# Bias, first weights and first gate sums between the token stage and the head stage of an audio tower kernel

## The reference

```python
x = layer_norm(x, g1, b1)                 # 1472 rows of 1024
h = layer_norm(x @ W + b, g2, b2)         # 1472 rows of 512, the residual
n = layernorm(h)
q, k, v = n @ Wq, n @ Wk, n @ Wv          # 8 heads, 2 queries for each key, width 128
log_g = log_sigmoid(6.9 + n @ Wg)         # a gate per token and head
logG = cumsum(log_g, over the tokens)
a = where(causal, (q.k * scale) ** 2 * exp(logG[t] - logG[s]), 0)
y = (a @ v) / (sum(a) + 1e-6)
h = h + y @ Wc + bc
```

## Time and profile before

| what | value |
|---|---|
| median of 3 runs | 1456.67 us (1453.85 to 1457.67) |
| profiled execution, its own time | 1465.22 us |
| its span in the profile | 1463.4 us |
| mean granted TensorE clock | 0.928 of full speed |
| VectorE, ScalarE, GpSimd busy | 63%, 44%, 16% |
| longest chain, by engine | TensorE 57%, VectorE 23%, issue 11% |

### The profile page before, as it was taken

The page is one execution under the profiler, slowest core; times in us unless marked ns, Lnnn a source line. Parts: engine busy times, 40 slices in busy tenths (PEclk is TensorE's granted clock), DMA queues, the critical chain, the costliest instruction groups (busy, mean ns, idle before and its releaser), DMA issues.

```text
span 1463.4 us, 28621 instructions
## 1 busy us (share of the span) xinstructions
PE 1293.8 (88%) x9676; PEld 796.9 (54%) x9690; DVE 916.6 (63%) x1920; ACT 638.8 (44%) x1086; POOL 230.1 (16%) x280
## 2 busy tenths in 40 slices
PE   5999899999999999986759999999986798759997
PEld 2447667677676766765324444444533566424443
DVE  5983565666555566659744555544347666678886
ACT  3444444544444454444215444444523432236663
POOL 2220000000000000000013333333257610010000
PEclk9997999999999999996769999999997877889999
DMA  5212352433535244322215866876346510000000
GB/s 187 72 65 86 119 205 105 179 146 127 215 135 195 99 173 163 130 111 90 86 73 196 293 225 249 297 249 202 102 140 117 89 26 3 1 0 16 22 22 26
DMA packets 42700, 184.21 MB, mean 126 GB/s; under 512 B 8689, under 2 KB 9201, under 8 KB 34833
## 3 DMA queue, kind: packets, MB, share of 16 engines
q0 software_dynamic: 19744, 95.41, 19.6%
q1 hardware_dynamic: 19440, 75.41, 14.5%
q10 hardware_dynamic: 3456, 12.58, 2.5%
HBM read 135.65 MB, written 47.73 MB: 125 GB/s over the span
## 4 chain that ended last, share of the span: by engine, by line
PE 57%; DVE 23%; issue 11%; ACT 3%; DMA 2%; DVEq 2%; POOL 1%; another core or an unknown queue 1%; ACTq 0%; SPq 0%; POOLq 0%
PE ps L911 14%; PE ps L913 14%; PE ps L912 14%; PE ps L1017 3%; PE ps L996 3%; DVE ff L2017 2%; DVE amf L2024 1%; PE ps L1033 1%; DVE wa_lo L1381 1%; PE ps L1101 1%; PE ps L1352 1%; DVE bst L1454 1%; PE ps L1334 1%; DVE nrm L1746 1%; PE ps L1002 1%
## 5 line engine op out<-in xcount | busy, mean ns | idle before, releaser
L911 PE MATMUL ps<-nT_hi,wa_hi 128*128 128x368 f16 x576 | 189.2, 328 | 11.1 <-DVE wa_lo L1381 8.1
L912 PE MATMUL ps<-nT_lo,wa_hi 128*128 128x368 f16 x576 | 188.9, 328 | 0.0
L913 PE MATMUL ps<-nT_hi,wa_lo 128*128 128x368 f16 x576 | 188.3, 327 | 0.0
L657 ACT ACTIVATE qk<-ps 128x368 f32<-128x368 f32 x128 | 60.4, 478 | 128.8 <-PE ps L913 128.6
L1746 DVE SCALAR_TENSOR_TENSOR nrm<-ps,xg,nrm 128x256 f32<-128x256 f32 x61 | 29.5, 484 | 133.1 <-ACT nrm L725 112.1
L911 PE MATMUL ps<-wide,xT 128*128 x244 | 93.4, 383 | 12.7 <-issue 7.5
L500 POOL DMA_INDIRECT xg<-xrow,idx x61 | 61.3, 1004 | 276.0 <-PE ps L1101 106.6
L1574 DVE TENSOR_TENSOR a<-sq,E 92x368 f32<-92x368 f32 x64 | 32.6, 537 | 107.2 <-ACT sq L673 107.2
L1548 DVE SCALAR_TENSOR_TENSOR wide<-ps,wide 128x368 f32<-128x368 f32 x128 | 69.4, 542 | 48.5 <-PE ps L913 48.5
L912 PE MATMUL ps<-wide,xT 128*128 x244 | 93.1, 382 | 0.0
L913 PE MATMUL ps<-wide,xT 128*128 x244 | 93.0, 381 | 0.0
(11 more groups left out here) (312 smaller groups left out, 3097.5 us busy)
## 6 DMA issues: line engine op xcount, KB each, us to landing
we_st<-in_we POOLq DMA_DIRECT2D x16, 1536.0 KB, 6.7
wsp<-we_sp POOLq DMA_DIRECT2D x16, 1536.0 KB, 5.3
wide<-wsp SPq DMA_DIRECT2D x16, 1536.0 KB
yslot<-yt POOLq DMA_DIRECT2D x61, 256.0 KB
wq_st<-in_ffq SPq DMA_DIRECT2D x24, 512.0 KB, 4.5
wq_st<-in_ffq ACTq DMA_DIRECT2D x24, 512.0 KB
wide<-in_wa SPq DMA_DIRECT2D x10, 1024.0 KB, 6.3
xt<-in_x SPq DMA_DIRECT2D x12, 512.0 KB, 3.2
```

Source lines behind the costliest of these rows:

```text
L657: nc.scalar.activation(B["qk"][:, j, :], ps[:, j % 2, 0:CW], ACT.Copy, scale=(AS if j == 3 else 1.0) / WS).then_inc(b_ev, 1)
L911: nc.tensor.matmul(dst, lhs[0], rhs[0], start=start, stop=False)
L912: nc.tensor.matmul(dst, lhs[0], rhs[1], start=False, stop=False)
L913: return nc.tensor.matmul(dst, lhs[1], rhs[0], start=False, stop=stop)
```

## The change

SyncE gets one more wait: it goes into the loop of loads only when the first gr has landed. ScalarE's four bias activations go behind turns 12 and 13 of the token pipeline, two in each, and each now counts up acc_set, so that VectorE waits for 4 (KD) in place of 1; the first weights' high half goes behind turn 14. VectorE's low half of these weights goes behind its turn 14 also, that is ahead of turn 15 with the last block's `ln_low`. TensorE forms the running sums of the gates after one projection of the first head in place of two.

```diff
--- before.py
+++ after.py
@@ -404,6 +404,7 @@
             sp.dma_start(lgd.rearrange("h (a p) -> (h a) p", p=AT), B["lgt"][:, :]).then_inc(init_out, 16)
             sp.wait_ge(init_out, 32)
             sp.dma_start(B["gr"][0:AT], lgd[0:1, :].broadcast_to([AT, T])).then_inc(gr_in, 16)
+            sp.wait_ge(gr_in, 16)
             with sp.Fori(0, HEADS - 1) as i:
                 sp.wait_ge(q_abs, 3 * i + 1)
                 for m in range(3):
@@ -637,14 +638,14 @@
                                      bias=A["nb"][:, 4 + p:5 + p], scale=rt_out[:, 4 + p:5 + p]).then_inc(ln_nr, 1)
 
 
+            def biased(b0, b1):
+                act.wait_ge(ones_set, 3)
+                for blk in range(b0, b1):
+                    nc.scalar.activation(big[:, blk, :], big[:, blk, :], ACT.Identity,
+                                         bias=bcol[:, blk:blk + 1]).then_inc(acc_set, 1)
+
             pipeline(act, NT, [(1, tok_high), (4, lambda k, p, half: ln_high(k, k, 4 + p)), (0, x_norm), (3, h_norm)],
-                     after={0: tok_weights})
-
-            unit_a_hi(0)
-            act.wait_ge(ones_set, 3)
-            for blk in range(KD):
-                ins = nc.scalar.activation(big[:, blk, :], big[:, blk, :], ACT.Identity, bias=bcol[:, blk:blk + 1])
-            ins.then_inc(acc_set, 1)
+                     after={0: tok_weights, NT: lambda: biased(0, 2), NT + 1: lambda: biased(2, KD), NT + 2: lambda: unit_a_hi(0)})
             act.wait_ge(g_mm, 2)
             nc.scalar.activation(B["lt"][0:AT, 1, :], B["lt"][0:AT, 1, :], ACT.Exp, scale=-1.0).then_inc(g_ln, 1)
             act.wait_ge(g_ln, 1)
@@ -1038,13 +1039,13 @@
                 out_proj(g, c)
 
             pe.wait_ge(wa_lo, 1)
-            for j in range(2):
-                head_project(0, 0, j)
+            head_project(0, 0, 0)
             pe.wait_ge(g_lg, 1)
             nc.tensor.matmul(ps[0:AT, 7, 0:16 * HEADS], tri[0:AT, :], B["lg"][0:AT].rearrange("p a b -> p (a b)"),
                              start=True, stop=True)
             nc.tensor.matmul(ps[:, 6, 0:AT], B["lg"][0:AT].rearrange("p a b -> p (a b)"), tri[0:AT, :],
                              start=True, stop=True).then_inc(g_cum, 1)
+            head_project(0, 0, 1)
             with pe.Fori(0, HEADS - 1) as i:
                 head(i, False)
             head(HEADS - 1, True)
@@ -1517,9 +1518,8 @@
             pipeline(dve, NT, [(3, z_stats), (0, x_stats(0)), (3, z_moments), (0, x_stats(1)), (0, x_moments), (3, z_scaled),
                                (0, shift(0, rx_done, a_sx)), (3, h_row), (1, x_low(0)), (3, h_stats), (1, x_low(1)),
                                (3, h_moments), (4, lambda k, p, half: ln_low(k, k, 4 + p)), (3, shift(2, rh_done, ln_st))],
-                     order, 8, after={0: tok_weights, 1: tok_bias})
-
-            unit_a_lo(0)
+                     order, 8, after={0: tok_weights, 1: tok_bias, NT + 2: lambda: unit_a_lo(0)})
+
             dve.wait_ge(consts_in, 16 * 13)
             dve.wait_ge(first_in, 48)
             order(V.tensor_copy(identb[:], ident[:]))
@@ -1538,7 +1538,7 @@
             order(V.tensor_copy(B["LG"][0:AT].rearrange("p a b -> p (a b)"), ps[0:AT, 7, 0:128]))
             order(V.memset(B["v1"][:, :, DH:DH + 1], 1.0))
             order(V.memset(asum[:], 0.0))
-            dve.wait_ge(acc_set, 1)
+            dve.wait_ge(acc_set, KD)
 
             def accumulate(g, c):
```

## The result

Over 20 runs of each kernel the changed one takes 1448.01 us (1445.14 to 1450.94) and the one before, measured again beside it, 1453.33 us (1448.37 to 1458.24). The ratio is 0.9964 with a 95% interval of 0.9954 to 0.9974, so 5.2 us less (3.8 to 6.7). Forecast were 7.5 us less, and 1449.2 us from the older median. In a later series one execution of the changed kernel took 1709.72 us at a mean granted clock of 0.729; it counts as slow and is left out of that series' ratio.

A forecast was written before the change was run, and what follows sets the result against it. TensorE, busy 88%, was taken as the bound, idling 6.7 us in the first head behind the gate sums' chain. Sums 2.17, spread 2.7 and clock 2.57 made 7.4 (7.5 by start times): 1456.67 to 1449.2 us, range 1445.8 to 1453.6.

The forecast's parts named there:

- The moved work of ScalarE and VectorE: Last token turns: bias activations and first weights' halves fit into slack there, at no cost; gates end at 133.3 us.
- The 0.3 us that I gave the second pair of biases: ScalarE, token turns: slack left between the second pair's end at 118.5 us and the next copy at 118.82.
- The sums: First head: running sums of gates behind 12 projection matmuls, not 24; VectorE's copy of them starts 2.17 us earlier.
- The spread: DMA of the gate sums from DRAM over 92 partitions: alone it takes 6.3 us, not 9.00; 2.7 us less.
- the 0.15 us for the completion: Added to the 6.15 us in which the lone transfer's last bytes are moved, giving 6.3 us.
- 1.3 us of idle is left: TensorE's remaining wait before the first head's product of weights and values: own work done 144.6, product at 145.9 us.
- the term of 2.57 us: TensorE's clock stays up after the shorter idle: product to second chunk's scores 8.02 us, not 10.59; bounds 0 and 2.57.
- Rival (b): Weights queued behind SyncE's wait come too late for ScalarE's absolute sum; 4 us given back, 1453.2 us; chance 0.05.
- Rival (a): The spread takes 9.0 us even without company; gain 2.2 us if the clock falls, 1454.5 us; chance 0.08.
- Rival (d): Small fp32 sums cut the projections and keep TensorE at 1.2 GHz; low till 161 us gives 1461 us; chance 0.04.
- Rival (c): Lone spread moves at 281 GB/s, lands within 4 us; TensorE bounds; gain 8.8 us, 1447.9 us; chance 0.05.
- (e): Something in the tail (routing, experts) absorbs 3 us or more of the gain; 1453.5 us; chance 0.05.

The follow-up runs named there:

- the order alone: Kernel before with only TensorE's part: running sums of gates after 12 projection matmuls in place of 24; single time 1453.93 us beside 1454.16 for the kernel before.

## Why the prediction was right, and where it was off

**The moved work of ScalarE and VectorE** cost nothing, as forecast, and it is there in the rows. The 0.3 us that I gave the second pair of biases was 0.49. The gates were ready before TensorE wanted them.

**The absolute time** was forecast as 1449.2 us and came as 1448.01. That nearness is partly luck: the older median of three runs lay 3.3 us above that of twenty, and the gain was forecast 2.3 us too high, and the two errors offset each other.

**The sums** were forecast 2.17 us earlier, and came 2.27 earlier by the raw times, 2.20 from the first projection. That it fits so closely is luck of the two profiles: the kernels with 24 projections ahead of the sums have 5.87 to 7.22 us there, those with 12 and early gates 3.98 to 4.67, means of 6.39 and 4.50, so 1.9 us. That ScalarE's part matters in this holds: with the order alone TensorE waited 1.5 us for the gates.

**The spread.** The difference of 2.7 us was right on the mean (9.61 and 6.85), but both ends were too low, and between the two first profiles it is only 1.9. With company the spread took 9.00 us in the one profile I had, and 9.48 to 10.06 in the five others with 92 rows; alone it took 6.57 to 7.08 in five executions, not 6.3. The step that was mis-sized is the 0.15 us for the completion, which I added to the last bytes without a row for it: from the last stretch of 0.2 us in which bytes move to the landing it is 0.5 to 0.6 us in all five, and that stretch ends 6.1 to 6.6 us after the issue. The write ahead of it, which I kept at 1.55, scatters from 1.53 to 2.48.

**The idle and the clock.** From these two, "1.3 us of idle is left" became 1.8 to 3.2 us; in the first profile 0.6 us of it are TensorE's own work, done just before 144 and not at 144.6. In one profile of three the clock then fell after all, and the term of 2.57 us shrank to 0.66 (9.93 us from L1018 to the scores against 10.59). Where the clock stays the term is 2.1 us and not 2.57, since I read it from the second head, where TensorE does not wait before the product: there it lasts 1.77 us and the scores follow after 8.02. After an idle of 0.5 to 2.3 us the product lasts 2.00 even where the clock stays, and the turning of its result is a quarter of a microsecond longer too. It is not the first head as such: with 96 rows and the wait TensorE does not idle, and the same two numbers are 1.77 and 8.02 there. So 7.5 us were forecast, D fell by 4.2, 6.7 and 6.1 us in three profiles, and the median by 5.2: the mechanism was right, the clock's term was mis-sized and taken as certain.

**The loads behind SyncE's wait** kept their slack: the absolute sum waits for nothing. Rival (b) is excluded. **Rival (a)**, the spread just as long alone, is excluded by the five executions alone against the six in company. **Rival (d)**, a clock that stays low because the sums cut the projections in two, did not come: the small sums ran at the low level, and the stretch from 138 to 143 us shows 1.00. (Its 26 us at the low level would have cost 13 us less the 8.8, so 4.2 and not 4.4.) **Rival (c)**, the spread at the rate of all engines, is false for 92 rows and true for 96. Nothing was absorbed later (e), as far as the interval can tell. The range of 1445.8 to 1453.6 us was said to hold (a) to (c), but the 1454.5 of (a) lies outside it.

The lone spread held a better idea already. The DMA engines are busy at a share of a quarter while it runs, in the second head of the kernel before as in the first of the changed one, and I used it for its duration only. By the Trainium skill, page DMA: Bandwidth & Descriptors, section Why a DMA increments its semaphore by 16 and not by 1, a DMA uses the largest number of engines up to 16 that divides the size of its slowest dimension, on both sides: 4 for 92, 16 for 96. The trace agrees with both: shares of 0.24 and 0.9, though a share is a mean over all 16 and does not tell which of them moved. The 3.2 us that the Trainium skill's page DMA: Bandwidth & Descriptors gives by the formula of its section Anatomy of one DMA — SWDGE (gpsimd) path were not reached even with 96 rows (3.97 and 3.99 us, with company).

ScalarE's table load of 1.28 us at 131.16 is followed by Ln at 132.46 without a gap, as in all 14 profiles. So the drain that the Trainium skill, page ScalarE: Activation LUTs, section What ACT_TABLE_LOAD costs, adds shows in no run here.

## What to carry to other kernels

A transfer on the path whose DMA share is a small fraction while it is alone should have its row count looked at before its company: from 92 to 96 rows gave more than clearing the queue beside it (ratios of 0.9958 and 0.9983 to the kernel before), and made the wait for an empty queue needless. Where a gain rests on an idle time falling below what lets the clock drop, count that part as a chance and not as a term; profile several executions, since a single one may lie at either end. And take the time of a transfer to the wait that it releases, not to its last byte.

## What the runs showed of the hardware that was not expected

- The same spread to 92 partitions uses a quarter of the DMA engines' time (share 0.24 from 138 to 143 us) and to 96 partitions 0.9, with nothing else changed: 6.57 to 7.08 us alone against 3.97 and 3.99 us beside loads, and 4.1 from its issue to the next where nothing runs beside it.
- TensorE's clock fell after idle times of 3.2, 4.3, 4.4, 5.9 (twice), 6.2, 6.7 and 7.4 us, and did not after 0.5, 0.9 (twice), 1.8 and 2.3 us. In the first profile of the changed kernel it fell only when TensorE was at work again (1.00 up to 148 us, L1018 having begun at 147.17).
- The price of such a fall is 1.4 to 3.1 us from the product to the next scores (9.92 to 11.54 us against 8.47 to 8.49), and does not follow the length of the idle alone: 4.3 and 4.4 us of idle gave 11.09 and 9.92.
- The clock's rise after the gate products shifts from one execution to the next: in the six that have 24 projections ahead of the sums and no wait for the gates, the copy of the sums starts 5.87 to 7.22 us after the first projection. That alone moves a single profile by a microsecond.
